# Four fused layers on one core: a token table that is gathered in place of slot rows that are scattered, and expert results written to four planes

## The reference, cut to what matters

```python
xn = rmsnorm(h, ln2_w)                          # h: 2048 tokens x 256
prob = softmax(xn @ gate_w.T)                   # 16 experts
w, e = top_k(prob, 4); w = w / w.sum(-1)        # four experts for each token
routed = sum over the four: w[k] * ((silu(g) * v) @ w2[e[k]].T),  g, v = split(xn @ w1[e[k]].T)
shared = (silu(xn @ sg.T) * (xn @ su.T)) @ sh_down_w.T      # 352 hidden channels, every token
out = x_before + tanh(g_ffn[1]) * (block output - x_before)
```

## Time and profile before

| | |
|---|---|
| median of 3 runs | 1984.11 us (1981.86 to 2006.73) |
| the profiled execution | 1989.11 us, span 1987.3 us |
| mean granted clock of TensorE | 0.922 |
| sort and shared expert | about 1609 to 1756 us |
| tile loop, its last scatter landed | about 1756 to 1966 us |
| planes, adds, stores | 1966.4 to 1987.3 us |

### The profile page before, as it was taken

One profiled execution on the slowest core, in us unless ns is written; L12 is line 12 of the kernel. 1 busy time (PEld: TensorE's weight loads), 2 busy tenths in 40 slices (PEclk: granted clock), 3 DMA queues, 4 the chain that ended last, 5 costly groups with the idle time before them and its releaser, 6 DMA issues. The chain is left out here.

```text
span 1987.3 us, 34326 instructions
## 1 busy us (share of the span) xinstructions
PE 1722.4 (87%) x11668; PEld 1455.4 (73%) x11668; DVE 1165.0 (59%) x2625; ACT 951.5 (48%) x2452; POOL 529.5 (27%) x527
## 2 busy tenths in 40 slices
PE   7998897697699999999992999999999969259993
PEld 6666664555688888888881788888888867258883
DVE  4688884698655656566546555555555457335553
ACT  2577776486355444545541444444454423225442
POOL 4133321243311111111111111111121114736663
PEclk7699997898899999999996999999999968679997
DMA  4111121265100100100002101001000043447666
GB/s 142 55 34 29 29 70 40 78 252 213 43 13 1 43 12 13 43 1 11 1 1 77 43 1 32 12 12 29 5 12 1 1 117 108 147 101 139 126 115 162
DMA packets 73274, 117.40 MB, mean 59 GB/s; under 512 B 8285, under 2 KB 59021, under 8 KB 71943
## 3 DMA queue, kind: packets, MB, share of 16 engines
q1 hardware_dynamic: 54014, 89.03, 14.4%
q0 software_dynamic: 14448, 19.80, 5.6%
q10 hardware_dynamic: 4648, 6.38, 1.0%
HBM read 86.65 MB, written 44.70 MB: 66 GB/s over the span
## 5 line engine op out<-in xcount | busy, mean ns | idle before, releaser
L1812 ACT ACTIVATE da_prob<-da_prob,da_nb,d_rqs 128x128 f32<-128x128 f32 x256 | 123.3, 483 | 260.2 <-DVE da_nb L2072 260.2
L1812 ACT ACTIVATE hold_wq<-hold_wq,ca_nb,c_rqs 128x128 f32<-128x128 f32 x256 | 123.4, 483 | 235.4 <-DVE ca_nb L2072 235.4
L653 DVE TENSOR_REDUCE a_mx<-a_s 128x2 f32<-128x512 f32 x256 | 167.1, 681 | 60.5 <-PE a_s L541 58.7
L470 ACT ACTIVATE a_prob<-a_s 128x512 f32<-128x512 f32 x256 | 147.4, 600 | 85.7 <-PE a_s L554 85.4
L1874 POOL TENSOR_TENSOR hold_wq<-hold_wq,ca_rsum 128x512 f32<-128x512 f32 x64 | 66.7, 1042 | 428.3 <-DVE ca_rsum L2077 428.3
L1874 POOL TENSOR_TENSOR da_prob<-da_prob,da_rsum 128x512 f32<-128x512 f32 x64 | 66.6, 1041 | 422.9 <-DVE da_rsum L2077 422.9
L2700 POOL DMA_INDIRECT slot_results<-t_ysb,t_dest x79 | 124.3, 1574 | 91.7 <-ACT t_ysb L2714 42.8
L554 PE MATMUL a_s<-a_qs,a_ks 32*128 32x256 f32 x512 | 101.6, 346 | 32.4 <-ACT a_prob L470 32.3
L1884 PE MATMUL da_qk<-d_xTh,da_wqkv_h 128*128 128x512 f32 x256 | 106.7, 417 | 6.4 <-DVE da_wqkv_l L2023 6.4
L541 PE MATMUL a_s<-a_ks,a_qs 32*128 32x256 f32 x512 | 101.0, 351 | 3.1 <-DVE a_mx L653 3.0
L2084 DVE SCALAR_TENSOR_TENSOR ca_oT_l<-ca_oT,ca_bv,ca_oT_h 128x512 fp32r<-128x512 f32 x64 | 48.0, 751 | 93.3 <-ACT ca_oT_h L1826 93.3
(11 more groups left out here) (412 smaller groups left out, 5610.2 us busy)
## 6 DMA issues: line engine op xcount, KB each, us to landing
t_xg<-slot_rows SPq DMA_DIRECT2D x79, 144.0 KB, 2.5
mw_raw<-in_d_expert_w SPq DMA_DIRECT2D x16, 352.0 KB, 6.1
slot_results<-in_d_fill SPq DMA_DIRECT2D x1, 4608.0 KB
a_heads<-a_osb SPq DMA_DIRECT2D x128, 32.0 KB
a_wraw<-a_heads SPq DMA_DIRECT2D x32, 128.0 KB, 2.1
mw_down<-in_d_expert_d SPq DMA_DIRECT2D x1, 2816.0 KB
hold_wk<-in_c_wkT SPq DMA_DIRECT2D x1, 2064.0 KB
hold_wq<-in_c_wqT SPq DMA_DIRECT2D x1, 2064.0 KB, 9.0
```

Source lines behind the costliest of these rows:

```text
L470: act.activation(prob[:, w % PR, :, :], s2[w % 2][:, :, :], ACT.Exp, scale=1.0 / A_ROOT)\
L653: dve.tensor_reduce(mx[:, b % 2, :, h], s1[s1_use(b, u) % S1_BANKS][:, :, :], AX.X, ALU.max)\
L1812: ins = act.activation(prob[:, p, b, :], prob[:, p, b, :], ACT.Exp, bias=nb[:, p, b:b + 1], scale=rqs[:, r:r + 1], accum_out=sums[:, p, b: ...
```

## The change

1. The blank fills at L787 and L790 go; one row of zeros is written to row 0 of a table of tokens in DRAM.
2. A row is 272 numbers (no token number). When the weights are in, SP stores `rows` (2048 rows) to the table behind row 0, in one plain DMA. The 64 scatters go.
3. The inverse of the sort, which token sits in each slot, is worked out on the chip. DVE turns the slot number into tile and lane (four small steps). For each batch (`locate`) it writes a 128 x 512 bfloat16 matrix that marks the lane and four 128 x 80 ones that hold a label in the tile's column; PE multiplies them, 64 products in all (`find`), and DVE decodes the sum (`identify`) into `ids` (the row to gather) and `dest` (where the result goes), for all 79 tiles at once. This is spread over the first four units of the shared expert.
4. POOL gathers tiles: 28 of them (`X_EARLY`) in the sort's block once `ids` is there, at most three in flight; 8 at the loop's start; 43 in the loop after the scatters, at most eight in flight. Together that is 51 outside the sort's block. SP's loads of tiles go. There are 44 tile buffers, in memory that the sort had used.
5. Each of a token's four results has a plane of its own, so a scatter writes plainly, waits for no earlier one, and nothing needs zeroing. `mask_meta`, `pick_meta` and `place` become one `tensor_tensor_reduce`.
6. At the end 16 pieces of 512 KB are loaded and added in place of 8; the loads of group n wait for the adds of group n-2, since two groups have buffers.
7. Experts 0 to 8 are split beside the units (the low parts in units 4 to 11), 9 to 11 beside the last `down`, 12 to 15 after it. The turned tokens are laid out by group, so that their memory comes free by groups. `silu` and `hid` are one buffer, and `gates(t)` waits for `rest_hid(t-2)`.

The diff, cut to its core:

```diff
@@ second layer, SP
-                sp.dma_start(slots.rearrange("(u r) n -> u r n", r=Y_BUFS * P),
-                             fill.unsqueeze(0).broadcast_to([TABLE // Y_BUFS, Y_BUFS * P, ROW])).then_inc(filled, 16)
...
+                sp.dma_start(slots[0:1, :], fill[0:1, :]).then_inc(filled, 16)
@@ constants
-META = 2 * EXPERTS
-ROW = DIM + META
+ROW = DIM + EXPERTS
+X_OWN, X_LOOSE = BATCHES, 16
+X_EARLY, X_AHEAD, X_BUFS = 28, 36, 44
+X_SEMS = 8
-EARLY = 5
+EARLY, SHARED, BEFORE = 5, 9, 12
-PLANES = 2
+PLANES = 4
@@ ExpertWeights
+    def fetched(self, eng, t):
+        eng.wait_ge(self.x_in[t % X_SEMS], 16 * (t // X_SEMS + 1))
+    def gather(self, pool, slots, t, behind):
+        if t >= behind:
+            self.fetched(pool, t - behind)
+        pool.indirect_dma_start(self.tile(t), None, slots[:, :],
+                                bass.IndirectOffsetOnAxis(self.ids[:, t:t + 1], 0)).then_inc(self.x_in[t % X_SEMS], 16)
@@ sort_and_share
+        SPLIT_HI = {6: 5, 7: 6, 9: 7, 10: 8}
+        SPLIT_LO = {4: (0, 1), 5: (2, 3), 6: (4,), 7: (5,), 8: (6,), 10: (7,), 11: (8,)}
@@ SP
+                sp.wait_ge(meta_ready, 1)
+                sp.wait_ge(xn_ready, BATCHES)
+                sp.dma_start(slots[1:1 + BATCHES * TOKENS, :].rearrange("(b p) c -> p b c", p=P), rows[:, :, :])\
+                    .then_inc(rows_stored, 16)
@@ POOL
-                for b in range(BATCHES):
-                    for k in range(TOPK):
-                        n = TOPK * b + k
-                        after(pool, sent_rows[n % IN_FLIGHT], 16 * (n // IN_FLIGHT))
-                        pool.indirect_dma_start(slots[:, :], bass.IndirectOffsetOnAxis(idx[:, b, k:k + 1], 0),
-                                                rows[:, b, :], None).then_inc(sent_rows[n % IN_FLIGHT], 16)
-                for k in range(IN_FLIGHT):
-                    pool.wait_ge(sent_rows[k], 16 * len(range(k, BATCHES * TOPK, IN_FLIGHT)))
+                pool.wait_ge(filled, 16)
+                pool.wait_ge(rows_stored, 16)
+                pool.wait_ge(turned_psum, PAIRS)
+                pool.wait_ge(ids_ready, 1)
+                for n in range(X_EARLY):
+                    first.gather(pool, slots, n, IN_FLIGHT)
@@ PE
+                def find(b):
+                    pe.wait_ge(lane_ready, b + 1)
+                    pe.wait_ge(named_ready, b + 1)
+                    for k in range(TOPK):
+                        mm = pe.matmul(f_ps, in_lane[:, b % DEEP, k, :], named[:, b % DEEP, k, :],
+                                       start=(b == 0 and k == 0), stop=(b == BATCHES - 1 and k == TOPK - 1),
+                                       skip_group_check=True)
+                    mm.then_inc(found_psum, 1)
...
                     if t == 1:
                         tally()
+                    if 1 <= t < 1 + GROUPS:
+                        find(GB * (t - 1))
+                        find(GB * (t - 1) + 1)
                     if t >= 2:
                         down(t - 2)
+                    if 1 <= t < 1 + GROUPS:
+                        find(GB * (t - 1) + 2)
+                        find(GB * (t - 1) + 3)
@@ ACT
+                act.wait_ge(u_psum, UNITS_S)
+                for n in range(SHARED, BEFORE):
+                    first.split_hi(act, big, n)
                 act.wait_ge(acc_psum, UNITS_S)
-                for n in range(EARLY, EXPERTS):
+                for n in range(BEFORE, EXPERTS):
@@ DVE
+                def locate(b):
+                    after(dve, found_psum, b - DEEP + 1)
+                    dve.tensor_tensor(in_lane[:, b % DEEP, :, :], lane_of[:, b, :].unsqueeze(2).broadcast_to([P, TOPK, P]),
+                                      lanes.unsqueeze(1).broadcast_to([P, TOPK, P]), ALU.is_equal).then_inc(lane_ready, 1)
+                    for k in range(TOPK):
+                        ins = dve.tensor_scalar(named[:, b % DEEP, k, :], times, tile_of[:, b, k:k + 1], cons[:, P + b + BATCHES * k:][:, 0:1],
+                                                ALU.is_equal, ALU.mult)
+                    ins.then_inc(named_ready, 1)
...
                 for t in range(UNITS_S):
                     hidden(t)
+                    if t < GROUPS:
+                        locate(GB * t)
+                        locate(GB * t + 1)
                     if t >= 1:
                         rest_hid(t - 1)
+                    if t < GROUPS:
+                        locate(GB * t + 2)
+                        locate(GB * t + 3)
+                    if t == GROUPS:
+                        identify()
@@ routed_experts
+        def rows_by(t):
+            return min(NT, X_AHEAD + (t + 1) * (NT - X_AHEAD) // (NT - X_SEMS - 1))
@@ SP
                 for n in range(GROUPS):
+                    after(sp, added, PLANES * (n - 1))
                     load_plane(sp, n, 0)
...
+                    load_plane(sp, n, 1)
+                    if n >= 1:
+                        store(n - 1)
@@ POOL
+                for t in range(X_EARLY, X_AHEAD):
+                    first.gather(pool, slots, t, X_SEMS)
                 for t in range(NT):
                     pool.wait_ge(y_copied, t + 1)
-                    pool.wait_ge(dest_ready, t + 1)
-                    if t >= PLANES:
-                        pool.wait_ge(sent[(t - PLANES) % Y_BUFS], 16 * ((t - PLANES) // Y_BUFS + 1))
...
+                    pool.indirect_dma_start(results[:, :], bass.IndirectOffsetOnAxis(first.dest[:, t:t + 1], 0),
+                                            ysb[:, t % Y_BUFS, :], None).then_inc(sent[t % Y_BUFS], 16)
+                    for n in range(rows_by(t - 1), rows_by(t)):
+                        after(pool, xT_psum, n - X_BUFS + 1)
+                        after(pool, picked, n - X_BUFS + 1)
+                        first.gather(pool, slots, n, X_SEMS)
@@ DVE
+                def pick_weight(t):
+                    first.fetched(dve, t)
...
+                    dve.tensor_tensor_reduce(weighed[:, t % 2, :], xg(t)[:, DIM:ROW], first.pick[:, t, :], 1.0, 0.0,
+                                             ALU.mult, ALU.add, wd[:, t % D_BUFS:t % D_BUFS + 1]).then_inc(picked, 1)
```

232 lines of the change are left out of this document (124 added, 108 removed).

## The result

The changed kernel takes 1971.39 us (median of 11 runs, 1969.25 to 1978.18), the kernel before 1993.23 us over the same number of runs: a ratio of 0.99, interval 0.9877 to 0.9922. The change gains 1%; the forecast was 1.8% (1949.2 us). The profiled execution took 1971.08 us with a span of 1969.0, 18.3 us less than the span before. The sum of the prediction had 34.9. In the medians the gain is 21.8 us.

The account below looks back on a forecast made before the run. POOL was taken to set the end of the sort's block, PE the tile loop's pace, DMA the end. -29.0 - 14.0 - 5.0 + 13.1 = -34.9 off a median of 1984.1 gave 1949.2 us, range 1933 to 1973.

Parts of the forecast that it names:

- the 28 gathers: Sort's block: gathers on POOL replace 64 scatters, 1.47 us a step, 40.7 us in all, ending at 1722.9.
- a gather at the plain scatter's price: POOL: a gather was taken to cost what a plain scatter does, 0.96 us and a gap of 0.30.
- the drain: After the loop's last result copy: 2.8 us to the first plane load in place of 7.8, 5.0 us less.
- The loop: Tile loop: 14.0 us of stalls, all given to the adding scatter, would go; PE's 2.27 us a tile stays.
- Rival D: Loop's stalls stay, since POOL and DMA load make them and POOL issues 122 times, not 79: +14, 1963 us; chance 0.08.
- B: Rival: a gather costs POOL what the adding scatter does, 1.85 us with its gap: 1967 us; chance 0.12.
- The sort: Sort's block: POOL starts 25.7 us later but PE's first tile comes at 1729.3, not 1758.27: 29.0 us less.
- The end: After the loop: twice the planes to load and add, 34.0 us against 20.9, 13.1 more; bounds 30 and 38.
- The rule that was set aside: Sort's block: by the skill's page, gathers would go at the quiet pace and the block end 3.4 us sooner.
- The 1.47: Sort's block: us per gather step, taken from the scatters' pace beside the shared expert (53/36); bounds 1.26 and 1.85.
- The blank fills: Removing the two fills was taken at nothing; a gain of a microsecond from less DMA was not excluded.

Follow-up runs that it names:

- a_static: Changed kernel with the loop's register loads taken out, each tile's expert a constant: 1963.21 us, ratio 0.9842 to the kernel before.
- before_again: The kernel before, unchanged, profiled again on a chip of the first kind: 1992.08 us, loop 196.0 us.
- b_static3: The kernel before with constant experts in place of the loop's register loads, on a chip of the first kind: 1991.17 us, loop 196.6 us.
- a_planes16: Changed kernel with a buffer for each of the 16 plane pieces, so no load waits for an addition: 1970.65 us, ratio 0.9885.
- a_two: Changed kernel reading and adding only two of four planes, each piece in its own buffer, on the second kind of chip: 1994.03 us, ratio 0.9964.
- after_third: The changed kernel itself, unedited, on the second kind of chip: 2012.9 us, ratio 1.0086 to the kernel before.
- a_acc: Changed kernel with an adding scatter in place of the plain one and the results' table zero-filled early, on the second kind of chip: 2304.4 us.
- a_early24: Changed kernel with 24 gathers ahead of the loop's barrier, not 28: 1968.55 us, ratio 0.9892.
- a_combo2: Changed kernel with 24 early gathers, 16 plane buffers, registers for 20 tiles and decoding ahead of the unit's two steps: 1969.3 us, ratio 0.9894.

## Why the prediction was wrong

Right were the direction, the 28 gathers (41.3 us measured, 40.7 said), a gather at the plain scatter's price (0.95 to 0.98), the drain (5.0), and that POOL ends the block. Of the 34.9 us, 16.6 did not come. Another 5 us of the miss of 22 (1971.4 for 1949.2) lie in the base. The profiled execution stood 5.0 above the median of three runs, and the prediction took these off; the median of eleven runs is 1993.23, 4.1 above that execution.

- **The loop, -14.0 said, -4.8 measured: the step that failed.** In the prediction's own measure, from the first copy to the last, 190.1 us became 186.3 and not 176.1. "They come from the adding scatter" took all stalls for one cause. In the trace of before, the steps at tiles 16, 32 and 64 took 3.8, 4.0 and 5.9 us and belonged to PE's register loads, `L2752 PEldq TENSOR_LOAD`, 10 of 1.1 to 1.8 us; the load at tile 48 fell together with a wait of ACT for a scatter, in steps of 5.1 and 3.1. The prediction asked what the waits of DVE were and not at which tiles the steps were long; the table of stretches with PE at 35.8 of 39 us sums over both. a_static shows these loads at 9.5 us in the changed kernel, and the pair before_again and b_static3 shows why nothing adds up in the kernel before: both limits held the loop at 196 to 200. The scatters' share was there, mostly at the four `KEEP` tiles, and it went; PE's stayed. Two profiles of the kernel before (199.9, 196.0) and two of the changed one (195.1, 193.7) put the gain at 3.6 us. Rival D ("the loop's stalls stay") came nearest in what it says, with another reason than it gave; B's 1967 came nearest as a number, without its dear gather.
- **The sort, -29.0 said, -25.35 measured**, of which 1.5 are an earlier start, no part of the change; from the sort's start it is 5.1 us short. The first gather came 6.9 us later on that scale: an 80-wide step with two scalars takes 0.23 and not 0.15, a `locate` 1.53 and not 1.2 (16 x 0.33 = 5.3), and `hidden(4)` and `rest_hid(3)` ahead of `identify` had been left out of the count (1.2). The gathers cost 0.6 more, and the next block began 4.0 us after POOL's end and not 6.4, which gave 2.4 back.
- **The end, +13.1 said, +16.8 measured.** 34.0 were forecast for 37.75, just within the bounds of 30 and 38. Groups 2 and 3 were asked for at 1943.5 and 1949.5, and the pause in front of the first add of group 2 is part of it: 2.8 us by a_planes16. The prediction had seen that wait, but let group 2's first data come 4.8 us after its load was asked for. Its first add started 7.9 us after (20.1 us after the first plane load, where 16.4 was said). The rate was 348 to 359 GB/s and not the 385 of the earlier trace rows. The Trainium skill's page "DMA: Bandwidth & Descriptors", section "Bandwidth", states about 358 GB/s for a core; the trace of the changed kernel agrees with that figure, and its 2 us belonged into the sum. But it is not the number of bytes that makes the difference, and the figure is no ceiling here: a_two moves as much as the kernel before and has 358, while all five profiles of the kernel before and its variants have 384 to 385 between the first add and the last. What lowered the rate stays open.
- **The rule that was set aside.** The Trainium skill's page "SBUF — State Buffer", section "Who interferes with whom", would have the gathers at the quiet pace of 1.26. 28 gathers and 27 gaps at the quiet 0.95 and 0.30 are 34.7 of the 41.3 us; POOL's busy time in 1687 to 1729 was 30.4, which is 3.8 above 28 x 0.95, with single gathers of up to 1.57. In this the trace disagrees with the rule, as the scatters' did. The other 2.8 us are waits for landings, since only three may be in flight (3.3 and 2.1 us in the line's list of waits, below, less the nine gaps of 0.30 that would be there anyway). The 1.47 held these waits without naming them.

```profile
  DMA mw_rows<-token_rows,mw_ids: 3.3, 7
  DMA mw_loose<-token_rows,mw_ids: 2.1, 2
```

- **The blank fills** at nothing: the sort's start lies within the spread of kernels that are alike up to there. Their removal shows no gain.

The range (1933 to 1973) held the 1971.4 by its upper end, which B's dearer gather had set. No gather was that dear, so this was luck. No rival had the second kind of chip, where the change is a loss (after_third).

## What to carry to other kernels

Before stalls are given to one cause, list the long steps of a loop by their index and hold them against everything in the program that happens every so many tiles: here every 16 (register loads) and every 10 (the scaling of `x_sb` and its load). Where two limits are of one size, removing one gains the distance to the other and no more; take each away alone (here constants for a table lookup) before pricing either. An end that only moves bytes goes by bytes over rate plus the waits for buffers. And a gain of 1% that rests on more indirect DMAs beside busy engines wants a look at several chips.

## What was not expected of the hardware

- Loading 32 offsets from SBUF into PE's registers stops PE for 1.5 us (a step of 3.8 for 2.28) as two loads of 1.1 to 1.8 us; at tile 64 a stop of 2.4 us was followed by some products at half clock (granted 0.50 in 1890 to 1892), which cost another 1.6 us. Without the loads the clock stayed at 1.00 in that stretch (a_static).
- On two of the five chips of these experiments, ACT and DVE stood still for 8 to 38 us with their inputs there, while POOL issued indirect DMAs. The changed kernel's loop was 24 us longer there and that of its variants with the plain scatter 30 to 35, and the change was a loss of 0.9%.
- In a_acc the zeroing of 8.9 MB in DRAM, one DMA of 1 KB rows, ran at 24 GB/s from 500 to 700 us of the span, and the load of `ctx` behind it was waited for 298 us.
- An adding scatter beside DVE's scaling of `x_sb` took 2.11 us of POOL in place of 1.55, and landed 5.0 us after its start in place of 3.9, or 5.9 to 6.5 where a 512 KB load followed (b_static3).
- PE's first product of the next block came 4.0 us behind POOL's end where POOL was last with its gathers (3.9 in a_early24), and 1.0 us behind DVE's end where DVE was last by 5 us (a_combo2).
